# Moving element-wise steps between VectorE, GpSimd and ScalarE in two attention blocks of an eight-part transformer kernel

## Time and profile before

| what | value |
|---|---|
| median of three runs | 1975.74 us (1969.93 to 1977.56) |
| profiled execution, its own time | 1987.75 us |
| its span in the trace | 1986.0 us |
| mean granted TensorE clock | 0.852 |
| busy: PE, DVE, ACT, POOL | 1622.9, 1170.6, 809.9, 616.7 us |
| first attention, main loop | about 79 to 297 us |
| third attention, quantizing block | about 932 to 972 us |
| third attention, main loop | about 972 to 1430 us |

### The profile page before, as it was taken

How to read it: one execution, slowest core, us unless ns; L and a number is a source line. 1 busy time by engine, 2 the same in 40 slices (tenths; PEclk the granted TensorE clock), 3 DMA queues, 4 the chain that set the end, 5 groups by cost and what they waited for, 6 DMA issues and landing times. The chain is left out here.

```text
span 1986.0 us, 25201 instructions
## 1 busy us (share of the span) xinstructions
PE 1622.9 (82%) x8472; PEld 1004.9 (51%) x8472; DVE 1170.6 (59%) x2652; ACT 809.9 (41%) x1871; POOL 616.7 (31%) x980
## 2 busy tenths in 40 slices
PE   6688878999786899995389898898699989737762
PEld 5323234556454455554166666666555565535542
DVE  5799972223554632425789999999822255553225
ACT  3888773111322211112377777777621112412221
POOL 0022211000200197900455555655210000036662
PEclk9755558999687899998699999999889988768886
DMA  2288871110501213111100000000101100245535
GB/s 72 52 161 161 159 149 62 40 40 17 170 1 59 104 59 125 52 52 33 53 1 1 1 1 1 1 1 1 41 20 40 40 23 1 111 156 204 207 126 224
DMA packets 174224, 140.12 MB, mean 71 GB/s; under 512 B 141793, under 2 KB 154721, under 8 KB 170386
## 3 DMA queue, kind: packets, MB, share of 16 engines
q1 hardware_dynamic: 165314, 114.89, 20.6%
q0 software_dynamic: 6416, 22.03, 3.3%
q10 hardware_dynamic: 2368, 1.61, 0.3%
HBM read 85.43 MB, written 19.50 MB: 53 GB/s over the span
## 5 line engine op out<-in xcount | busy, mean ns | idle before, releaser
L1417 PE MATMUL l2x_pr<-l_w,l2x_xq 128*128 128x512 bf16 x576 | 141.1, 383 | 41.0 <-ACT credits L42 40.5
L350 PE MATMUL l1e_gu<-x_normT,l1e_w 128*128 128x512 f32 x384 | 170.8, 599 | 0.0
L1875 ACT ACTIVATE l0m_pf<-l0m_s,l0m_bias,l0x_sq 128x1024 int16<-128x1024 f32 x128 | 154.1, 1204 | 38.9 <-POOL l0m_bias L1807 38.9
L1901 DVE TENSOR_REDUCE l0m_mx<-l0m_s 128x1 f32<-128x1024 f32 x128 | 155.8, 1219 | 21.8 <-PE l0m_s L1817 20.3
L1817 PE MATMUL l0m_s<-l0x_kT,l0x_qT 48*128 48x512 bf16 x256 | 126.1, 620 | 35.9 <-ACT l0m_pf L1875 31.8
L350 PE MATMUL l0e_gu<-x_normT,l0e_w 128*128 128x512 f32 x272 | 121.5, 601 | 0.0
L1807 POOL TENSOR_SCALAR l0m_bias<-l0m_mx,l0x_nsq 128x1 f32<-128x1 f32 x128 | 46.7, 365 | 225.1 <-DVE l0m_mx L1901 222.3
L350 PEld LDWEIGHTS l1e_gu<-x_normT,l1e_w 128*128 128x128 f32 x384 | 73.8, 193 | 83.8 <-issue 82.8
L350 PE MATMUL l2e_gu<-x_normT,l2e_w 128*128 128x512 f32 x256 | 114.4, 602 | 0.0
L1546 DVE TENSOR_SCALAR l2x_raw<-l2x_raw,l2x_mv,l2x_rs 128x128 f32<-128x128 f32 x384 | 111.2, 351 | 3.5 <-POOL l2x_rs L1396 3.3
L1417 PEld LDWEIGHTS l2x_pr<-l_w,l2x_xq 128*128 128x128 bf16 x576 | 56.6, 99 | 96.3 <-ACT credits L42 40.7
(11 more groups left out here) (515 smaller groups left out, 3636.8 us busy)
## 6 DMA issues: line engine op xcount, KB each, us to landing
l3m_w<-in_l_moe SPq DMA_DIRECT2D x16, 1280.0 KB
l1e_w<-in_l_ffn SPq DMA_DIRECT2D x24, 384.0 KB, 3.1
l_rows<-zero_row SPq DMA_DIRECT2D x8, 1024.0 KB, 11.1
l_w<-l_rows SPq DMA_DIRECT2D x8, 1024.0 KB, 11.8
l0e_w<-in_l_ffn SPq DMA_DIRECT2D x17, 384.0 KB, 3.0
l2e_w<-in_l_ffn SPq DMA_DIRECT2D x16, 384.0 KB, 3.1
ctx_tok<-l_route SPq DMA_DIRECT2D x8, 512.0 KB
l2q_wps<-in_l_wp SPq DMA_DIRECT2D x16, 256.0 KB, 2.7
```

Source lines behind the costliest of these rows:

```text
L350: last = nc.tensor.matmul(gu[half][:, m, :], w[:, c % SW, (2 * k + m) * P:(2 * k + m + 1) * P], pg.xnT[:, k, cols(n)], start=(k == 0), sto ...
L1417: last = nc.tensor.matmul(flat(pr[t % 2][:]), src[:, k, tokens], pg.l2_w3[:, part, k, at:at + W], start=(k == 0 and part == 0), stop=(k == ...
L1875: nc.scalar.activation(pf[:, n % 4, :], s_ps[n % 3][:], ACT.Exp, scale=sq[:, b, h:h + 1], bias=bias[:, n % 4:n % 4 + 1], accum_out=sm[:, b ...
L1901: nc.vector.tensor_reduce(mx[:, n % 4:n % 4 + 1], s_ps[n % 3][:], AX, ALU.max).then_inc(s["maxed"], 1)
```

## The change

In the first attention the integer copy moves to GpSimd, directly behind the exponential, and the bias to VectorE, behind the maximum. In the third attention `quantize` becomes `widen`, without the last step and with the step multiplied by 1.5 x 2^20 in the clamp (whose upper bound of 256 goes); the last step is a subtraction on GpSimd in both blocks. `step` and `wide` get two buffers, `cq` four, the new semaphore `widened` takes the place of `rounded` and `quanted` where only VectorE's part is waited for, and the projection of a group moves from lag 8 to 9. The weights are converted by ScalarE, two pieces after each division, from four load buffers.

```diff
@@ def quantize, now widen
-def quantize(nc, ch, z, step, wide, out):
+def widen(nc, ch, z, step, wide):
     v = nc.vector
     ch.link(v.tensor_scalar(step.bitcast(I16), z.bitcast(I16), 0x7F80, None, ALU.bitwise_and))
-    ch.link(v.tensor_scalar(step, step, 2.0 ** -6, 256.0, ALU.max, ALU.min))
-    ch.link(v.scalar_tensor_tensor(out=wide, in0=step, scalar=1.5 * 2.0 ** 20, in1=z, op0=ALU.mult, op1=ALU.add))
-    return v.scalar_tensor_tensor(out=out, in0=step, scalar=-1.5 * 2.0 ** 20, in1=wide, op0=ALU.mult, op1=ALU.add)
+    ch.link(v.tensor_scalar(step, step, 2.0 ** -6, 1.5 * 2.0 ** 20, ALU.max, ALU.mult))
+    return v.tensor_tensor(wide, step, z, ALU.add)
@@ attention_l2, quantizing block
-            wps = sb("wps", [P, 2, 2, D])
+            wps = sb("wps", [P, 4, 2, D])
...
             def _(sp):
                 for q in range(16):
-                    if q >= 2:
-                        sp.wait_ge(wp_kept, q - 1)
-                    sp.dma_start(wps[:, q % 2], pg.dram["l2_wp"][:, 2 * q:2 * q + 2, :]).then_inc(wp_in[q % 2], 16)
+                    if q >= 4:
+                        sp.wait_ge(wp_kept, q - 3)
+                    sp.dma_start(wps[:, q % 4], pg.dram["l2_wp"][:, 2 * q:2 * q + 2, :]).then_inc(wp_in[q % 4], 16)
             def _(act):
+                def keep(q):
+                    act.wait_ge(wp_in[q % 4], 16 * (q // 4) + 16)
+                    nc.scalar.activation(wp[:, 2 * q:2 * q + 2, :], wps[:, q % 4], ACT.Copy).then_inc(wp_kept, 1)
...
                 for n, (k, j) in enumerate(jobs):
                     if n >= 2:
-                        act.wait_ge(rounded, n - 1)
+                        act.wait_ge(widened, n - 1)
...
+                    for q in range(2 * n - 2, 2 * n):
+                        if q >= 0:
+                            keep(q)
+                keep(14)
+                keep(15)
             def _(pool):
-                for n in range(len(jobs)):
-                    keep(2 * n)
-                    keep(2 * n + 1)
+                for n, (k, j) in enumerate(jobs):
+                    pool.wait_ge(widened, n + 1)
+                    nc.gpsimd.tensor_tensor(xq[:, j, k, :], wide[:, n % 2], step[:, n % 2], ALU.subtract).then_inc(rounded, 1)
             def _(dve):
...
-                    quantize(nc, ch, z[:, u], step[:, u], wide[:, u], xq[:, j, k, :]).then_inc(rounded, 1)
+                    widen(nc, ch, z[:, u], step[:, u], wide[:, u]).then_inc(widened, 1)
@@ attention_l2, main loop
-            step = sb("step", [P, U, P], BF16)
+            step = sb("step", [P, 2, U, P], BF16)
-            wide = spare[:, 1024:1536].rearrange("p (u n) -> p u n", u=U)
+            wide = spare[:, 1024:2048].rearrange("p (a u n) -> p a u n", a=2, u=U)
-            cq = sb("cq", [P, 2, U, P], BF16)
+            cq = sb("cq", [P, 4, U, P], BF16)
...
             def _(pool):
                     for t in range(8):
+                        if job := due(t, 7, ai, zi):
+                            _, a, m = job
+                            pool.wait_ge(s["widened"], m + 3)
+                            nc.gpsimd.tensor_tensor(cq[:, a], wide[:, a % 2], step[:, a % 2], ALU.subtract).then_inc(s["quanted"], 1)
...
             def _(pe):
-                        if job := due(t, 8, ai, zi):
+                        if job := due(t, 9, ai, zi):
...
             def _(act):
                         if job := due(t, 5, ai, zi):
-                            act.wait_ge(s["quanted"], m + 1)
+                            act.wait_ge(s["widened"], m + 1)
...
             def _(dve):
                         if job := due(t, 6, ai, zi):
-                            dve.wait_ge(s["quanted"], m + 2)
+                            dve.wait_ge(s["widened"], m + 2)
+                            dve.wait_ge(s["quanted"], m + 1)
...
-                            quantize(nc, ch, z[:], step[:], wide, cq[:, a % 2]).then_inc(s["quanted"], 1)
+                            widen(nc, ch, z[:], step[:, a % 2], wide[:, a % 2]).then_inc(s["widened"], 1)
@@ attention_l0, main loop
             def _(pool):
                 for n in range(N):
-                    b, h = divmod(n, H)
-                    pool.wait_ge(s["maxed"], n + 1)
-                    if n >= 4:
-                        pool.wait_ge(s["exped"], n - 3)
-                    nc.gpsimd.tensor_scalar(bias[:, n % 4:n % 4 + 1], mx[:, n % 4:n % 4 + 1], nsq[:, b, h:h + 1], float(np.log(255.0)),
-                                            ALU.mult, ALU.add).then_inc(s["biased"], 1)
+                    pool.wait_ge(s["exped"], n + 1)
+                    if n >= 8:
+                        pool.wait_ge(moved[n % 8], 16 * (n // 8))
+                    nc.gpsimd.tensor_copy(pi[:, n % 8, :], pf[:, n % 4, :]).then_inc(s["rounded"], 1)
             def _(dve):
                 def top(n):
...
-                def rounding(n):
-                    dve.wait_ge(s["exped"], n + 1)
-                    if n >= 8:
-                        dve.wait_ge(moved[n % 8], 16 * (n // 8))
-                    nc.vector.tensor_copy(pi[:, n % 8, :], pf[:, n % 4, :]).then_inc(s["rounded"], 1)
+                    dve.wait_ge(s["maxed"], n + 1)
+                    if n >= 4:
+                        dve.wait_ge(s["exped"], n - 3)
+                    nc.vector.tensor_scalar(bias[:, n % 4:n % 4 + 1], mx[:, n % 4:n % 4 + 1], nsq[:, b, h:h + 1], float(np.log(255.0)),
+                                            ALU.mult, ALU.add).then_inc(s["biased"], 1)
...
-                    if 0 <= n - 2 < N:
-                        rounding(n - 2)
```

More of the change, by code:

```diff
@@ L1246, in attention_l2 @@
         cols, scales = pre.tiles
-        lnt, inverse, divided, steps, rounded, wp_kept = (
-            pg.sem(f"l2q_{m}") for m in ("ln_affine", "inverse", "divided", "steps", "rounded", "wp_kept"))
-        wp_in = [pg.sem(f"l2q_wp_in{i}") for i in range(2)]
+        lnt, inverse, divided, steps, widened, rounded, wp_kept = (
+            pg.sem(f"l2q_{m}") for m in ("ln_affine", "inverse", "divided", "steps", "widened", "rounded", "wp_kept"))
+        wp_in = [pg.sem(f"l2q_wp_in{i}") for i in range(4)]
         with ExitStack() as st:
@@ L1303, in _ @@
                     ch.link(nc.vector.tensor_scalar(z[:, u], z[:, u], 448.0, -448.0, ALU.min, ALU.max))
-                    quantize(nc, ch, z[:, u], step[:, u], wide[:, u], xq[:, j, k, :]).then_inc(rounded, 1)
+                    widen(nc, ch, z[:, u], step[:, u], wide[:, u]).then_inc(widened, 1)
         names = ("const", "proj", "raw", "stats", "eps_in", "rstd", "normed", "ln_turned", "affined", "scores", "maxed", "exped",
-                 "recip", "p_normed", "p_turned", "p_kept", "valued", "o_read", "qsteps2", "quanted", "y_done", "y_added", "aff_in", "aggr", "y_scale", "smooth")
+                 "recip", "p_normed", "p_turned", "p_kept", "valued", "o_read", "qsteps2", "widened", "quanted", "y_done", "y_added", "aff_in", "aggr", "y_scale", "smooth")
         s = {m: pg.sem(f"l2x_{m}") for m in names}
@@ L1461, in fn @@
                                 first, final = side == 0 and a == 0 and j == 0, side == 1 and a == 3 and j == U - 1
-                                last = nc.tensor.matmul(y[:, 0:D], cq[:, a % 2, j, :], wp[:, side * 16 + a * U + j, :], start=first, stop=final)
+                                last = nc.tensor.matmul(y[:, 0:D], cq[:, a, j, :], wp[:, side * 16 + a * U + j, :], start=first, stop=final)
                             if side == 1 and a == 3:
@@ L1518, in _ @@
                 pg.credit(nc.vector, s["quanted"], 2)
+                pg.credit(nc.vector, s["widened"], 2)
                 for c in range(4):
@@ L1527, in _ @@
                 dve.wait_ge(s["y_scale"], 1)
-                QSTEPS = 4
+                QSTEPS = 3
                 def fn(pi, ai, zi):
@@ L1897, in top @@
                 def top(n):
+                    b, h = divmod(n, H)
                     dve.wait_ge(s["scores"], n + 1)
```

3 lines of the change are left out of this document (removed).

## The result

| | before | after |
|---|---|---|
| median of four runs | 1976.65 us | 1960.69 us (1958.64 to 1962.16) |
| profiled execution, its own time | 1987.75 us | 1962.16 us |
| its span | 1986.0 us | 1960.4 us |

The ratio is 0.9938, with a 95% interval from 0.9915 to 0.9961: 12 us faster, about half of the 25 us that were forecast. The medians lie 16 us apart, and so do the stages that the change touches. The two profiled executions lie further apart, 25.6 us in span, because of the last stage, which the change does not touch (16.6 us, last column).

A forecast was written before the change was run, and what follows sets the result against it. VectorE was taken to bound the first attention and quantizing block, VectorE and TensorE nearly full in the main loop. -15 + 3 - 13 = -25 us takes 1987.75 to 1962.75, 1950.7 as median of runs; range 1922 to 1984.

The forecast's parts named there:

- First attention, -15: First attention's loop: moving the copy off VectorE and the bias onto it saves 15 us of a possible 16.6.
- the value product (about 1 us every fourth head) delays somewhat more than now. I take 15 of the 16.6 us: First attention's loop: TensorE's value product was expected to take only a little of the 16.6 us saving, leaving 15.
- Quantizing block, +3: Third attention's quantizing block: the lock keeps GpSimd's subtraction from running beside VectorE, costing 3 us; bounds -12 to +4.
- 2.62 + 2.13 + 0.1 = 4.85: Quantizing block, us per job: VectorE's 2.62, then GpSimd's subtraction 2.13 + 0.1 alone; eight jobs take 38.8.
- Main loop, -13: Third attention's main loop: VectorE loses 58 us of rounding, less 34 and 11 for waits; bounded by 38 saved, +25 lost.
- rival B: Main loop: the lock eats the gain, late subtractions falling on the normalization; 1964 us, up to 1975; chance 0.18.
- TensorE reads the product one step later than before, with four buffers; that costs only at the end of the loop, under 3 us: Main loop: TensorE's later step was counted only as a cost at the loop's end, under 3 us.
- A: Main loop: the lock rarely bites and TensorE's idle time is used up, 41 us saved there; 1923 us; chance 0.14.
- C: First attention: the integer copy costs GpSimd 2.13 us, each head 2.23, +75 us, in all 2041; chance 0.10.
- D: Main loop: GpSimd is full, its 6.3 us a pair stretched by locks to 7; +26, in all 1992; chance 0.07.
- E: First attention: VectorE's bias waits for a gap between copies, head 1.41 us, 6 us less saved; 1957; chance 0.05.
- three signs of being wrong: Copy over 1.4 us, quantizing block below 30 us, or TensorE's idle time in the main loop not falling.

The follow-up runs named there:

- run 7: Changed kernel with the first attention's value product issued in two halves, output steps unchanged; first loop 210.8 us, ratio to the kernel before 0.9911.
- run 8: Changed kernel with the first attention's value product in two halves and output steps spread apart; first loop 208.6 us, ratio to the kernel before 0.9889.
- run 5: Changed kernel with the quantizing block's subtraction back on VectorE, weight conversions staying on ScalarE; block 32.0 us, ratio to the kernel before 0.9902.
- run 13: Changed kernel, main loop's subtraction on VectorE with the new formula, buffers and lag 8 as before; main loop 460.3 us, ratio to the kernel before 0.9952.
- run 14: Changed kernel, main loop's old formula wholly on VectorE, second buffers and lag 9 kept; main loop 450.8 us, ratio to the kernel before 0.9904.
- run 16: Changed kernel, main loop's subtraction on VectorE, four `cq` buffers and lag 9, single `step` and `wide` buffers; one execution, main loop 451.1 us.
- run 10: Changed kernel with only the main loop's subtraction put back on VectorE; main loop 450.3 us, ratio to the kernel before 0.9918.
- run 4: Changed kernel with the main loop's GpSimd subtraction replaced by a 128x8 power on other tiles; one execution, main loop 440.9 us.

## Why the prediction was right and wrong

*First attention, -15, measured -6.4.* This is the term that failed most, in two places. The copy on GpSimd took 1.04 us (forecast 1.04), the bias 0.214 us (0.165), and the spacing became 1.38 us (1.34): the saving was 0.09 us a head and not 0.13, 11.5 us in 128 heads and not 16.6. Then the step "the value product (about 1 us every fourth head) delays somewhat more than now. I take 15 of the 16.6 us" failed: TensorE's value product and output steps kept 5.1 us, where I had allowed 1.6. I had the row for it, four heads at 6.09 us against 4 x 1.47 = 5.88, and should have written out all 16 spacings: where TensorE sets the spacing, a faster VectorE gains nothing. Runs 7 and 8 show it, since splitting that product returns 5.7 and 7.9 us.

*Quantizing block, +3, measured -0.4.* The lock came as forecast, full length in every job. The step that failed is the sum 2.62 + 2.13 + 0.1 = 4.85, which laid subtraction and VectorE's work end to end: the held operation contains its own 0.43 us and ends only 0.28 after the subtraction, and the subtraction starts 0.16 us into the clip, so that most of the clip lies beside it. The measured job is 4.32. Run 5 shows what was missed in the other direction: 3.78 without GpSimd.

The Trainium skill, "SBUF — State Buffer", section "SBUF: two separate sides", has the exclusive lock held for the whole instruction; the block agrees (2.23 us for an operation of 0.43, ending 0.28 after GpSimd's 2.24).

*Main loop, -13, measured -9, for another reason.* The balance of VectorE was right in kind: I gave 34 + 11 us back to the lock; measured in the window of 380 us are 36 on the normalization (342 x (458 - 354) ns) and 11 on the widening, less 10 that the clamp no longer waits. (Half of 1.13 is 0.565, so the 34 should have read 36.) Most of the loss falls on the normalization, which only rival B named. But this balance did not set the time. The step that failed is "TensorE reads the product one step later than before, with four buffers; that costs only at the end of the loop, under 3 us": I gave no gain to the edit that wins the whole 9 to 10 us without the move (runs 13, 14, 16). Rival B, the lock eating the loop's gain, is what happened to the move itself at lag 9 (run 10 against after: nothing left). B's time, 1964, is what the ratio makes of the forecast's base (0.9938 x 1975.74 = 1963.5), but by luck: B has -15 + 3 + 0 where the stages gave -6.4, -0.4 and -9.1.

*Rivals.* A, C, D and E fell: the lock bites, the copy is not at 2.13 us, GpSimd is not full (281 of 390 us), and no bias is held by a copy. In the plain stretch the bias starts after each copy's end (98.90 + 1.04 = 99.94, the next bias at 100.06), but where TensorE delays a maximum it meets one:

```profile
103.04 1.04 POOL L1811 CAST l0m_pi<-l0m_pf 128x1024 bf16<-128x1024 int16 x1 [0.34 <-ACT l0m_pf L1878]
103.16 0.21 DVE L1909 TENSOR_SCALAR l0m_bias<-l0m_mx,l0x_nsq 128x1 f32<-128x1 f32 x1
```

Of the 128 biases 37 overlap a copy, and all 128 take 0.212 to 0.215 us. Beside E the prediction names the Trainium skill, "VectorE: DVE Perf Modes", section "What auto-detection actually checks", by which a one-source SBUF operation of the right sizes takes both ports; the bias shows no sign of it here. Whether it is the bias or the copy that leaves the ports free, no run tells. Two figures of the rivals do not follow from their terms: E's loss is (1.41 - 1.34) x 128 = 9 us and not 6, and D's -15 + 3 + 26 gives 1990 and not 1992.

*Signs.* None of the three signs of being wrong appeared: the copy takes 1.04 us, the block 36.8, and TensorE's idle time in the main loop fell from 38 to 28 us (390 - 362.19). The sign that did miss is the four heads, 5.86 us where I said 5.5 to 5.7.

*Sum.* -15 + 3 - 13 = -25 against -6.4 - 0.4 - 9.1 = -16 by stages, and -12.2 by the ratio (interval -7.7 to -16.8). Direction and range held; the size did not, because of the first attention's term. The main loop's term came near by luck, since what it counted won nothing and what it left out won the time.

## What to carry to other kernels

Before an engine is relieved, write out the spacing of its main operation over a whole period: only the intervals that it sets itself can shrink, and the others tell which engine to split next. Work given to GpSimd beside VectorE's SBUF operations can cost VectorE as much as it took over, so the move needs a run against leaving it out. And an edit that changes only *when* an in-order engine takes its input deserves a term of its own, and a run of its own, before the larger edit beside it gets the credit.

## What was not expected of the hardware

The TensorE clock in the step behind the first loop differed between runs without any change there. Windows of the changed kernel, and of run 5, whose first attention is the same:

```profile
300.00:316.00 16.00, 13.34 (x51) 11.11 (x52) 6.09 (x26) 6.80 (x14) 0.15 (x1) 0.50 0.35 121
```

```profile
300.00:316.00 16.00, 13.39 (x54) 9.84 (x55) 8.26 (x51) 6.80 (x14) 0.15 (x1) 0.62 0.35 120
```

Where the granted clock stays at 0.50, the 1.2 GHz level, the step takes 15.2 us, otherwise 12.4 to 12.9. Both happened with one first attention, so 2.3 us of a comparison of two profiles can be this alone.

A power of 128x8 on GpSimd (1.64 us) does not hold VectorE as a subtraction of 128x512 (1.16 us) does: with it in that place VectorE's widening keeps its 693 ns (run 4). The trace of the kernel before shows the same of the power in its statistics chain: 14 exponent-bit operations that run wholly beside one take 0.293 to 0.296 us, and 50 normalizations 0.329 to 0.345, while the 20 exponent-bit operations that start during a multiply take 1.01. And VectorE's maximum, which reads PSUM, stays at 1.21 to 1.23 us under every one of GpSimd's 1.04 us copies; its batch-norm statistics, which read SBUF, take 0.27 to 0.29 us even beside a subtraction.
